# Joining the first two head groups of the 14-wide attention layers before the output projection, and scaling the last group in two steps

## The reference

```
# layers 0 and 2: windows of 14 x 14 (the 16 x 16 image is padded), 12 heads of 16
# layer 1: one window of 16 x 16, 12 heads of 48
q, k, v = layer_norm(x) @ w_qkv + b_qkv               # by head
attn    = softmax(scale * q @ k.T + rel_h + rel_w)    # per window and head
out     = (attn @ v).reshape(tokens, heads * head_dim) @ w_proj + b_proj
x       = x + out
x       = x + gelu(layer_norm(x) @ w1 + b1) @ w2 + b2
# layer 3
y       = irfft2(softshrink(mlp(rfft2(x)))) + x
```

## Time and profile before

| | |
|---|---|
| median of 3 runs | 605.55 us (603.67 to 606.29) |
| profiled execution | 607.03 us, of which span 605.2 us |
| mean granted clock of PE in the span | 0.952 of 2.4 GHz |
| PE busy | 530.5 us, 88% |
| DVE busy | 296.9 us, 49% |
| ACT busy | 229.4 us, 38% |
| POOL busy | 139.7 us, 23% |

### The profile page before, as it was taken

How to read it: one execution, slowest core, us unless ns; L and a number is a source line. 1 busy time by engine, 2 the same in 40 slices (tenths; PEclk the granted TensorE clock), 3 DMA queues, 4 the chain that set the end, 5 groups by cost and what they waited for, 6 DMA issues and landing times.

```text
span 605.2 us, 10070 instructions
## 1 busy us (share of the span) xinstructions
PE 530.5 (88%) x3840; PEld 382.5 (63%) x3840; DVE 296.9 (49%) x776; ACT 229.4 (38%) x453; POOL 139.7 (23%) x206
## 2 busy tenths in 40 slices
PE   6968889899988958878888999979879897999997
PEld 4726768674764545455666694756467675848676
DVE  4735866563143552655757452136566755711142
ACT  4304544535335116254544405333235446250210
POOL 8003000103005055073472216020030101120030
PEclk9979998899998979999989999989989898999999
DMA  6893547003312635616637205502916420020001
GB/s 169 190 196 72 118 103 254 1 3 96 94 58 59 134 96 134 155 47 145 145 89 173 114 1 127 123 20 57 192 43 144 92 92 2 2 67 0 1 0 53
DMA packets 21863, 55.39 MB, mean 92 GB/s; under 512 B 4560, under 2 KB 10248, under 8 KB 21688
## 3 DMA queue, kind: packets, MB, share of 16 engines
q1 hardware_dynamic: 21432, 54.65, 37.4%
q0 software_dynamic: 384, 0.10, 0.1%
HBM read 12.28 MB, written 0.79 MB: 22 GB/s over the span
## 4 chain that ended last, share of the span: by engine, by line
PE 62%; DVE 16%; SPq 8%; ACT 5%; DMA 5%; issue 4%; DVEq 0%; ACTq 0%
PE PS L1267 59%; DVE NM L1163 5%; DVE REL L1148 3%; DMA QA<-REL 2%; PE PS L1283 2%; SPq L745 2%; SPq L737 2%; ACT REL L992 2%; SPq L755 1%; DMA PT<-in_qm 1%; SPq L693 1%; ACT OT L953 1%; ACT KD L953 1%; DVE OT L1195 1%; DVE HL L1173 1%
## 5 line engine op out<-in xcount | busy, mean ns | idle before, releaser
L1163 DVE TENSOR_REDUCE NM<-PS 98x2 f32<-98x392 f32 (+2 forms) x192 | 105.7, 569 | 87.4 <-PE PS L1267 86.1
L1012 ACT ACTIVATE PT<-PS 98x392 f32<-98x392 f32 (+2 forms) x192 | 95.5, 518 | 79.0 <-PE PS L1267 77.7
L1267 PE MATMUL PS<-KA,QA 128*98 128x196 f32 (+3 forms) x432 | 90.9, 306 | 27.7 <-DVE NM L1163 22.5
L1267 PE MATMUL PS<-QA,KA 128*98 128x196 f32 (+2 forms) x480 | 91.9, 295 | 10.5 <-ACT PT L1012 5.7
L1267 PEld LDWEIGHTS PS<-KA,QA 128*98 128x98 f32 (+3 forms) x432 | 65.0, 189 | 54.6 <-DVE NM L1163 30.1
L1267 PEld LDWEIGHTS PS<-QA,KA 128*98 128x98 f32 (+2 forms) x480 | 72.9, 191 | 22.6 <-issue 12.4
L1267 PE MATMUL PS<-NR,SEL 128*98 128x392 f32 x144 | 54.4, 378 | 0.6 <-DVE NR L1185 0.6
L1267 PE MATMUL PS<-XT,WQKV 128*128 128x512 f32 (+3 forms) x104 | 49.0, 734 | 6.4 <-issue 3.3
L1267 PE MATMUL PS<-XT,W 128*128 128x512 f32 (+1 forms) x144 | 51.6, 614 | 0.0
L1267 PEld LDWEIGHTS PS<-W,HT 128*128 128x128 f32 x288 | 46.6, 190 | 4.5 <-ACT HT L1033 2.3
L1148 DVE TENSOR_TENSOR REL<-PS,REL 32x512 fp32r<-32x512 f32 (+5 forms) x64 | 28.5, 480 | 42.7 <-ACT REL L992 42.3
(11 more groups left out here) (108 smaller groups left out, 703.0 us busy)
## 6 DMA issues: line engine op xcount, KB each, us to landing
QA<-QHL SPq DMA_DIRECT2D x36, 192.0 KB
KA<-KHL SPq DMA_DIRECT2D x24, 228.0 KB
QA<-REL SPq DMA_DIRECT2D x24, 224.0 KB
QA<-QHL SPq DMA_DIRECT2D x12, 384.0 KB
KA<-KHL SPq DMA_DIRECT2D x12, 384.0 KB
KA<-PT SPq DMA_DIRECT2D x12, 380.0 KB
QA<-REL SPq DMA_DIRECT2D x24, 128.0 KB
W<-in_w SPq DMA_DIRECT2D x3, 768.0 KB, 4.4
```

Of the source, the lines that this page charges most:

```text
L1012: nc.scalar.activation(dst, src, ACT.Exp).then_inc(probs_done.sem, 1)
L1163: nc.vector.tensor_reduce(dst, src, AX.X, ALU.max, negate=True).then_inc(max_done.sem, 1)
L1267: return nc.tensor.matmul(dst, lhsT, rhs, start=start, stop=stop, skip_group_check=loose)
```

## The change

In the 14-wide layers a new step `merge` follows `weights` on SP's list. SP waits until the second group is scaled (`o_done`), and then four transfers move the 16 value rows of each of its four heads into rows 16 to 31 of the same slot in the first group, over the row of sums and the zeros. The weights are packed in the same way: `WP` has two tiles instead of three (`out_tiles`), the first one for eight heads, and the bias goes to the last tile. The first part of a projection step is then one matmul instead of two, and it waits for the transfers (`merged`) instead of for `o_done`.

In all three blocks `norm` for half 1 now does only the two transposes and the reciprocal. Its product is a new step `scale`, behind `ln` of tiles 0 to 3. As bank 7 is free only after it, the first part of tile 7 moves behind `turn`.

```diff
+        self.out_tiles = self.groups - (head_dim == 16)
...
-                out.append(("weights", 0, 0, 0))
+                out += [("weights", 0, 0, 0), ("merge", 0, 0, 0)]
...
-    out += [("proj", t, 0, t) for t in range(4, TILES)]
-    out += [("ln", 1, 0, 0), ("turn", 1, 0, 0)]
+    out += [("proj", t, 0, t) for t in range(4, TILES - 1)]
+    out += [("ln", 1, 0, 0), ("scale", 1, 0, 0), ("turn", 1, 0, 0), ("proj", TILES - 1, 0, TILES - 1)]
...
+            elif step == "merge":
+                sp.wait_ge(*o_done.at(n, 2 * L.groups - 3))
+                for first in range(0, 128, L.slot):
+                    sp.dma_start(m["OT"][first + L.hd:first + L.slot, 0, :], m["OT"][first:first + L.hd, 1, :])\
+                        .then_inc(merged.sem, 16)
...
-            elif step == "norm":
+            elif step in ("norm", "scale"):
...
+                if step == "norm":
+                    link(nc.vector.transpose(turned, o))
+                    link(nc.vector.reciprocal(inv, sums[:, :, L.sum_row]))
+                    link(nc.vector.transpose(rows, inv.unsqueeze(2).broadcast_to([128, 16, 32])))
+                    if i:
+                        continue
...
+                tiles = (L.out_tiles - 1,) if u else range(L.out_tiles - 1)
+                if u:
+                    pe.wait_ge(*o_last.at(n, t // 4))
+                elif L.pads:
+                    pe.wait_ge(*merged.at(n, L.per_group - 1))
+                else:
+                    pe.wait_ge(*o_done.at(n, 2 * tiles[-1] + t // 4))
+                for w in tiles:
+                    g = L.groups - 1 if u else w
+                    last = mm(PS[:, bank, 0:C], m["OT"][:, g, t * 128:(t + 1) * 128], m["WP"][:, w, :],
+                              w == 0, w == L.out_tiles - 1)
...
-        place[0, L.sum_row, 0] = bp
+        if L.pads:
+            place[:, L.hd:, 0] = place[:, :L.hd, 1]
+            place = place[:, :, ::2].copy()
+        place[0, L.sum_row, L.out_tiles - 1 if L.pads else 0] = bp
```

More of the change, by code:

```diff
@@ L460, in _build @@
         frame = ExitStack()
-        m["WP"] = sb(frame, f"WP{n}", [128, L.groups, C])
+        m["WP"] = sb(frame, f"WP{n}", [128, L.out_tiles, C])
         attn = ExitStack()
@@ L570, in _build @@
     o_done = count("o_done", per(lambda L: 2 * L.groups - 2))
+    merged = count("merged", per(lambda L: L.per_group if L.pads else 0), 16)
     o_last = count("o_last", [2, 2, 2, 0])
@@ L1207, in _ @@
                 inv = m["SUMS"][:, 0, i * 16:(i + 1) * 16] if L.pads else m["SUMS"][:, i, 0:16]
-                link(nc.vector.transpose(turned, o))
-                link(nc.vector.reciprocal(inv, sums[:, :, L.sum_row]))
-                link(nc.vector.transpose(rows, inv.unsqueeze(2).broadcast_to([128, 16, 32])))
+                if step == "norm":
[4 more added lines that the diff above has]
+                        continue
                 pieces = [(m["OT"][:, L.groups - 1, i * 512:(i + 1) * 512], o, rows)]
@@ L1617, in _pack @@
             rb[:, i, 1, :, i] = rw.T
-        arrays |= {f"col{n}": col, f"wqkv{n}": deep(wqkv), f"wp{n}": place.reshape(128, L.groups, C),
+        arrays |= {f"col{n}": col, f"wqkv{n}": deep(wqkv), f"wp{n}": place.reshape(128, L.out_tiles, C),
                    f"rb{n}": rb.reshape(CK, 2, L.rel, L.per_chunk), f"w1_{n}": deep(w1),
```

## The result

| | before | after |
|---|---|---|
| median of 22 runs each | 607.03 us (597.53 to 614.84) | 608.24 us (604.42 to 613.75) |
| mean of the same runs, with its standard error | 607.26 ± 0.98 us | 608.94 ± 0.58 us |
| profiled execution (its span) | 607.03 us (605.2) | 607.94 us (606.0) |
| mean granted clock of PE | 0.952 | 0.946 |

The measured ratio is 1.0081, with a 95% interval of 1.0052 to 1.011: slower, by less than 1%. It leaves out every run over 1.5% above its kernel's fastest, which is 11 of the 22 runs of before (fastest 597.53) and one of the 22 of after, while the means further down leave out only one run of 873 us (e10) and one of 764 us (e11). So I set the means of all 22 runs beside it, whose ratio is 1.0028 (0.9992 to 1.0064). Every ± is a standard error. By the ratio the change costs 4.9 us, by the means 1.7. The forecast was +2.2 us and 607.7.

A forecast was written before the change was run, and what follows sets the result against it. The prediction took DVE to bound the stage before the MLP in 14-wide layers: 0.4 us saved, 2.6 lost to clock falls behind PE's hole, net +2.2 on a median of 605.55, so 607.7 us; range 605.5 to 609, overall 603.5 to 610.

The forecast's parts named there:

- What bounds the stage: Between attention and MLP in layers 0 and 2: DVE sets the end, PE idles 0.43 us for its normalised tile.
- PE's saved matmuls: Projection, two 14-wide layers: 5.2 us saved on PE but turned into idle time; rival that all counts: 600.3, chance 0.05.
- at 0.33 us each: DVE's four additions after the projection: from 131.81 on at this pace, each finding its tile closed by PE.
- 0.2 are left: Gain at the MLP's start per 14-wide layer: of DVE's 0.75 us, 0.2 remain after tile 7's late part.
- The hole: PE's idle time ahead of the transposes in layers 0 and 2: 2.75 us where 0.43 stood.
- The chance of a fall, three in four: Behind the hole in each 14-wide layer: PE's clock drops to 1.2 GHz with this chance.
- a clock that holds in both layers: Rival for the stage in layers 0 and 2: clock stays at 1.00, 0.4 us gained, 605.1; chance 0.18.
- The price, 1.3 us (0.4 to 1.7): Loss per 14-wide layer from 3.4 us at low clock: 0.4 on transposes, 0.9 on projection and MLP.
- The rival of a stretch twice as long: Low clock behind the hole lasts double, 1.7 us more per layer: 609.4 or 611.1; chance 0.12.
- Transfers and layer 1: Merge landed by 124, PE wants it at 129.32: zero cost; layer 1 zero; late-transfers rival 609 to 611, chance 0.04.
- The sum: Whole kernel: saved 2 x 0.2 = 0.4, lost 2 x 1.3 = 2.6, net +2.2 us.
- a microsecond each way: Run-to-run allowance in the forecast's range of 605.5 to 609, from times of before differing by 2.6 us.

The follow-up runs named there:

- e10: Kernel of before with idle matmuls in PE's other holes, run again on the first chip; ratio to before 0.9982, mean 603.9 us.
- e11: Changed kernel with seven dummy matmuls in the hole ahead of the transposes and idle matmuls in PE's other holes; ratio to before 0.9941, mean 601.4 us.
- e3: Changed kernel with undivided scaling and tile 7 back in place, so only transfers and two-tile projection remain; 610.45 us, ratio to before 1.0095.
- e4: Changed kernel without transfers, with three groups; only the two-step scaling and the moved tile 7 remain; 608.86 us, ratio to before 1.0053.
- e1: The changed kernel again, no edit, beside before on one chip; median 610.77 us, ratio to before 1.0113.
- e9: Changed kernel with idle matmuls in PE's other holes but none in the hole ahead of the transposes; ratio to before 0.9979, mean 604.5 us.
- e5: Transfers and their waits alone: PE still multiplies three groups, moved rows meet zero weights, scaling undivided; 605.14 us, ratio to before 0.9965.
- e2: Changed kernel with seven dummy matmuls of 128 x 192 in the hole ahead of the transposes; 607.32 us, ratio to before 1.0033.
- e6: Changed kernel with four dummy matmuls in the hole ahead of the transposes in place of seven; 605.62 us, ratio to before 0.9992.
- e7: Kernel of before with idle matmuls in PE's other holes; 604.74 us, ratio to before 0.9962, mean 604.7 us.

## Why the prediction was right in its mechanism and wrong in size

*What bounds the stage.* DVE did, as read: PE's saved matmuls came out as idle time, ended by DVE's normalised tile, and the time did not drop by 5.2 us. But the pace that it gave the additions, "at 0.33 us each", was not DVE's own. In the earlier trace rows four additions take 1.33 us, so one starts every 0.325 us, which is PE's pace for two records (2 x 0.164). In the trace of before PE closes the four tiles at 132.52, 132.84, 133.17 and 133.49, and each addition starts 0.04 us behind. In after the tiles are closed between 130.78 and 131.76, the additions do find them closed, and they start every 0.27 us (four in 1.15 us; in e3 the same without the moved products). So in before PE paced them without an idle mark, and DVE alone did not set the end; e4 shows it, where DVE without the products at once waits 0.85 us for PE.

*The gain, "0.2 are left".* Measured 0.39 in a layer, in every stage where the clock held (11.31 or 11.32: two with the hole open, eight with it filled or halved). The missing 0.17 us is, within 0.01, the 0.18 that the merge gives the additions. This is a term of the sum that was mis-sized.

*The hole.* 2.44 and 2.42 us for 2.75: DVE came 0.18 us earlier, and PE's 22 records ended 0.13 later.

*The chance of a fall, three in four.* The open hole stood in six profiled stages (after, e1, e9): four fell, two held. With it filled or halved, none of eight did. The working gave 0.18 to a clock that holds in both layers, where two chances of one in four give 0.06 if they are independent; six stages cannot tell.

*The price, 1.3 us (0.4 to 1.7).* The four falls moved the MLP by 1.39, 1.10, 1.45 and 1.11 us past the held 11.31, 1.26 on average. In layer 0 of after, 0.40 of 1.39 is on the transposes and 0.99 on the projection; the working had 0.4 and 0.9. The Trainium skill (TensorE: Matmul & The Clock Gate, "HAM oscillation — how this bites in real kernels") charges half of the time at the low level. The fall in layer 0 of after had 3.41 us of it in the records, which makes 1.71 an estimate by the page; all four measured less. How much less goes with where the low stretch begins: 0.12 and 0.13 us behind the first transpose it cost 1.10 and 1.11 us, 0.71 behind it 1.39, and 1.04 behind it 1.45. So the part that falls on transposes waiting for DVE costs little, as the working had it; for a fall at their start its 1.3 was 0.2 too much. The rival of a stretch twice as long did not come in these four, which were 3.4 us each; in e3 it came once.

*Transfers and layer 1.* Both at nothing, as forecast (e5; 18.19 against 18.20). The landing was earlier than worked out, 118.4 for 124: POOL had the second group scaled at 114.05 in that execution and not at 117.48, one issue takes 0.59 us and not 0.85, and the last transfer lands 2.4 us behind its issue.

*The sum.* By the measured terms two layers give 2 x (1.26 x 4/6 - 0.39) = +0.9 us on average, and 2 x (1.26 - 0.39) = +1.7 where both fall, as in the profiled execution. The forecast had +2.2, with both layers falling for certain, though it gave each three chances in four; weighted so, its own terms give 2 x (0.75 x 1.3 - 0.2) = +1.6.

*The step that failed* is the one that gave the rest of the kernel nothing in the sum and a microsecond each way in the range: "Times of before differ by 2.6 us between runs, so I allow a microsecond each way." Those were three runs. In 115 runs before takes 597.5 to 617.3 us, and 20 of them lie under 603.29, the shortest of 28 runs of after. In the 93 that stand beside e1 to e11 the time follows the time at the low level with a correlation of 0.95: 588.6 us, plus 0.30 us for each microsecond there. Before spends 60.9 ± 1.3 us at the low level and after 68.5 ± 1.5 (28 runs), 7.5 ± 2.0 more, worth 2.3 us; at an equal time there, after is 0.47 ± 0.31 us *faster*, which agrees with the 0.8 of the two stages. Together +1.8 us, which is what the means give: 609.0 ± 0.5 for after, 607.2 ± 0.4 for before. That agrees with the forecast's +2.2, and it is less than half of the 4.9 us of the ratio.

How much the clock elsewhere moves one and the same program, two executions show. The profiled one of after (span 606.0 us) spends 65 us at the low level, 7 of them in the two falls; that of e1 (601.5) spends 47, 3 of them in its one fall. So 58 and 43 us lie outside the two stages, where before's profiled execution has 58 as well. The spans differ by 4.5 us, of which the stages account for 1.0. The other 3.5 go with 15 us less at the low level elsewhere, in one and the same program, and that is as much as the part of the 4.9 which the means do not show.

What stays open is the rest of the ratio, some 3 us over the +1.8. Of the 7.5 us more at the low level the stages account for 2 x 3.41 x 4/6 = 4.5; the other 3 are worth 0.9 us and no run shows the change causing them. With the hole filled no cost is left (e2 and e6 together 0.8 ± 0.8 us below before). So the rest of the ratio is most likely scatter in kernels whose runs spread by up to 3%, but that it is chance is argued, not shown.

## What to carry to other kernels

Taking work from an engine that then waits is not free: look at how long its wait becomes and whether the clock falls behind it, and put idle matmuls in the hole if it does (here a fall cost 1.1 to 1.5 us of the stage). A merged row without an idle mark can still be paced by another engine: divide its length by its count and compare that with the same instruction elsewhere. Before forecasting a difference below 1%, know the scatter of the kernel over many runs and what it follows; three runs do not tell.

## What the runs showed of the hardware that was not expected

The times of before scatter by 20 us and go with the time at the low level (correlation 0.95), and holes that no one had counted as a cost are worth several microseconds. With idle matmuls in some of them, and no other edit, before's mean falls by 3.2 ± 1.2 us (e7) and 3.7 ± 1.0 (e10). With the change as well (e11) the time is 0.9941 of before (0.9903 to 0.9978), and the mean clock of the profiled execution goes from 0.946 (after) to 0.979 (over all runs from 0.944 to 0.970):

```profile
core 0: 606.0 us, clock 0.946
```
```profile
core 0: 596.1 us, clock 0.979
```

At 0.30 us each, the 61 us at the low level would cost before 18 us, 3% of its time. This is an estimate: no run comes near a full clock throughout, and the idle matmuls, which took 23 and 24 us of the low level away, gave back half of that rate. The Trainium skill (TensorE: Matmul & The Clock Gate, "What's actually happening") puts the ramp at less than 1% of a typical kernel's span; here the low level comes back again and again, and the estimate is three times that. And the same hole, 2.42 us in e1 and 2.43 in e9, left the clock alone in one layer and not in the other of a single execution, so a single profile can't tell whether a hole costs.
